# Layer 0's ternary feed-forward: a turn over five batches, the up product scaled on ScalarE, the norm weight on GpSimd

## What is computed

```python
def activation_quant(x):
    s = 127 / clip(max(abs(x), axis=-1), EPS)
    return clip(round(x * s), -128, 127) / s

def weight_quant(w):
    s = 1.0 / clip(mean(abs(w)), EPS)
    return clip(round(w * s), -1.0, 1.0) / s

def bit_linear(x, w):
    return einsum('bsh,oh->bso', activation_quant(x), weight_quant(w))

h = silu(bit_linear(x, w_gate)) * bit_linear(x, w_up)      # 1024 columns
h = ln_weight * (h * rsqrt(mean(h * h) + RMS_EPS))
return bit_linear(h, w_down)                               # 256 columns
```

## Time and profile before

| | |
|---|---|
| median of 3 runs | 3764.42 us (3761.03 to 3766.98) |
| the profiled execution | 3751.3 us, of which its span is 3749.5 |
| busy over the span: PE / DVE / ACT / POOL | 83% / 65% / 43% / 10% |
| mean granted clock of TensorE | 0.91 of full speed |
| tile of the gated product in the stage | first 763.8, last 983.1 us |

### The profile page before, as it was taken

The page is one execution under the profiler, slowest core; times in us unless marked ns, Lnnn a source line. Parts: engine busy times, 40 slices in busy tenths (PEclk is TensorE's granted clock), DMA queues, the critical chain, the costliest instruction groups (busy, mean ns, idle before and its releaser), DMA issues. The chain is left out here.

```text
span 3749.5 us, 77344 instructions
## 1 busy us (share of the span) xinstructions
PE 3113.6 (83%) x28592; PEld 2241.5 (60%) x28592; DVE 2427.6 (65%) x6361; ACT 1617.8 (43%) x3972; POOL 378.5 (10%) x443
## 2 busy tenths in 40 slices
PE   7899999744487898999999999287999679976898
PEld 6566666411265556656666666165887676765786
DVE  6655555588677666666667666776788228856662
ACT  2243444377443455555555555032334224433341
POOL 3000000000042111111111111000110000000110
PEclk9899999855598899999999999598788899999899
DMA  2000000000320000000000000300000000000803
GB/s 99 31 16 23 16 23 15 2 0 0 110 54 2 2 1 3 1 3 1 1 3 1 1 3 1 97 1 6 17 14 9 0 0 1 0 25 21 223 35 105
DMA packets 97026, 90.80 MB, mean 24 GB/s; under 512 B 17680, under 2 KB 85840, under 8 KB 96336
## 3 DMA queue, kind: packets, MB, share of 16 engines
q1 hardware_dynamic: 90656, 79.78, 7.2%
q10 hardware_dynamic: 5808, 7.41, 0.6%
q0 software_dynamic: 384, 1.05, 0.1%
HBM read 79.83 MB, written 8.39 MB: 24 GB/s over the span
## 5 line engine op out<-in xcount | busy, mean ns | idle before, releaser
L3118 PE MATMUL bank<-L1w_w,L1x_xqT 128*128 128x512 f32 x640 | 304.5, 599 | 2.1 <-DVE L1x_xqT L3386 2.1
L3392 DVE TENSOR_REDUCE L1x_ssq<-L1x_square 128x4 f32<-128x512 f32 x192 | 131.5, 685 | 185.7 <-ACT L1x_square L3245 179.8
L1046 DVE TENSOR_REDUCE L0x_top<-bank 128x4 f32<-128x512 f32 x256 | 159.1, 683 | 102.6 <-PE bank L972 99.5
L1031 ACT ACTIVATE L0x_P<-bank,L0x_level 128x512 f32<-128x512 f32 x256 | 155.1, 688 | 156.1 <-PE bank L992 156.1
L3344 POOL TENSOR_TENSOR L1x_square<-L1x_square,L1x_total 128x512 f32<-128x512 f32 x128 | 133.2, 1041 | 603.7 <-DVE L1x_total L3420 603.7
L888 DVE TENSOR_TENSOR x_sb<-x_sb,bank 128x256 f32 (+1 forms) x112 | 47.0, 420 | 223.4 <-PE bank L208 179.9
L3269 ACT ACTIVATE L1x_square<-bank,L1x_top 128x128 f32<-128x128 f32 x512 | 182.0, 375 | 19.7 <-DVE L1x_top L3414 19.7
L3179 PE MATMUL bank<-L1w_wp,L1x_catb 128*128 128x256 bf16 x1536 | 188.4, 273 | 0.1
L3245 ACT ACTIVATE L1x_square<-bank 128x512 f32<-128x512 f32 x192 | 114.8, 598 | 146.8 <-PE bank L3118 146.8
L3118 PEld LDWEIGHTS bank<-L1w_w,L1x_xqT 128*128 128x128 f32 x640 | 115.4, 192 | 99.4 <-issue 95.2
L3179 PEld LDWEIGHTS bank<-L1w_wp,L1x_catb 128*128 128x128 bf16 x1536 | 150.2, 98 | 35.3 <-issue 17.1
(11 more groups left out here) (655 smaller groups left out, 7616.1 us busy)
## 6 DMA issues: line engine op xcount, KB each, us to landing
L0x_mask<-in_maskrows SPq DMA_DIRECT2D x16, 512.0 KB, 3.5
L3f_wgu<-in_L_ffn_Wg SPq DMA_DIRECT2D x8, 704.0 KB, 9.0
L3f_wgu<-in_L_ffn_Wu SPq DMA_DIRECT2D x8, 704.0 KB, 10.2
L1a_wp_quarter<-in_L_xattn_wproj SPq DMA_DIRECT2D x4, 1024.0 KB, 5.6
L3x_ctxT<-in_ctxT SPq DMA_DIRECT2D x32, 128.0 KB, 2.1
L3f_wd<-in_L_ffn_Wd SPq DMA_DIRECT2D x8, 512.0 KB, 9.1
turned_sends<-L3r_sendT ACTq DMA_DIRECT2D x16, 256.0 KB, 2.0
L3e_sends<-turned_sends SPq DMA_DIRECT2D x16, 256.0 KB, 2.9
```

The costliest lines, as they stand in the source:

```text
L1031: act.activation(self.P[:, i % 2, r, :], self.work_bank[r][:, :], ACT.Exp, bias=self.level[:, :]).then_inc(self.p_ready.sem, 1)
L1046: dve.tensor_reduce(self.top[:, s, 16 * c + 4 * r:16 * c + 4 * r + 4], self.work_bank[r][:, :].rearrange("p (h k) -> p h k", h=4), X, ALU.max,
L3118: last = pe.matmul(made_bank[n % 4][:, :], inputs(SOURCE[n], k), w[:, k, 4 * n:4 * n + 4, :], start=(k == 0), stop=(k == C - 1))
L3392: dve.tensor_reduce(ssq[:, 4 * n:4 * n + 4], square[:, (n + 2) % 3, :].rearrange("p (h e) -> p h e", h=4), X, ALU.add).then_inc(sum_ready. ...
```

## The change

TensorE, ScalarE, VectorE and GpSimd now each run `turn(t)` for t from -2 to 17, in which up to five batches (t - 2 to t + 2) are under way. Two turns make a loop's body, four lie on either side.

- VectorE's turn: h of t, the residual of t - 2, the norm and rounding of t - 1, `prepare` of t + 2.
- ScalarE's turn: squares of t, two exponentials and two scaled copies of t + 1, the copy of the turned hq of t - 1, the gate's logarithm (t + 1), the logarithm of the mean square (t), the gate's last exponential (t + 1), the exponential that makes the inverse root (t), and the copy of the turned q of t + 2.
- TensorE's turn: gate and up of t + 1, turning and down product of t - 1, turning of q of t + 2.
- The up product is scaled by ScalarE as it is copied out of its banks. The product with the norm weight is GpSimd's, from h into one of two buffers (`hl`). The root no longer multiplies h: it goes into the scale with which h is rounded and into the largest value. Root and reciprocal become a logarithm and an exponential.
- The sums of absolute weights move to ScalarE, all three in front; the last batch's norm is finished ahead of the weights.

```diff
...
+class TernaryHalves(Ternary):
+
+    def sum_scalar(self, act):
+        act.activation(self.q[:, :, :], self.raw[:, :, :], ACT.Abs, accum_out=self.total[:, :]).then_inc(self.summed, 1)
+    def vector(self, dve, step, out, guard, eps):
+        dve.wait_ge(self.spread, 1)
+        step(dve.tensor_scalar(self.unit[:, :], out, 1.0 / self.count, eps, ALU.mult, guard))
+        step(dve.reciprocal(self.scale[:, :], self.unit[:, :]))
+        step(dve.tensor_scalar(self.raw[:, :, :], self.raw[:, :, :], self.scale[:, :], 1.0, ALU.mult, ALU.min))
+        step(dve.tensor_scalar(self.raw[:, :, :], self.raw[:, :, :], -1.0, ROUND, ALU.max, ALU.add))
+        step(dve.tensor_scalar(self.q[:, :, :], self.raw[:, :, :], ROUND, None, ALU.subtract))
...
-        wg, wu, wd = Ternary(ph, "wg", C, F, weights), Ternary(ph, "wu", C, F, weights), Ternary(ph, "wd", FC, D, weights)
+        wg, wu, wd = TernaryHalves(ph, "wg", C, F, weights), TernaryHalves(ph, "wu", C, F, weights), TernaryHalves(ph, "wd", FC, D, weights)
...
+        unit, unit_g = ph.sb("unit", [128, 2]), ph.sb("unit_g", [128, 2])
+        gate, up, sig, h = (ph.sb(n, [128, F]) for n in ("gate", "up", "sig", "h"))
+        hl = ph.sb("hl", [128, 2, F])
+        ssum, rms, newton = ph.sb("ssum", [128, 2]), ph.sb("rms", [128, 2]), ph.sb("newton", [128, 1])
...
+        gate_exp, gate_log, up_kept = ph.batch_sem("gate_exp", 2), ph.batch_sem("gate_log"), ph.batch_sem("up_kept", 2)
+        product_made = ph.batch_sem("product_made", 2)
...
+        FIRST, LAST = -2, B + 2
+        def turns(eng, turn):
+            for t in range(FIRST, 2):
+                turn(t, t % 2, t)
+            with eng.Fori(0, (B - 4) // 2) as i:
+                for odd in range(2):
+                    turn(i * 2 + (2 + odd), odd, 2 + odd)
+            for t in range(B - 2, LAST):
+                turn(t, t % 2, t)
+        live = lambda t: 0 <= t < B
...
                 if not first:
-                    pe.wait_ge(banks_read.sem, banks_read.after(b - 1))
+                    pe.wait_ge(product_made.sem, product_made.after(b - 1))
...
-            front(0, first=True)
-            with pe.Fori(0, B - 1) as b:
-                front(b + 1)
-                back(b)
-            back(B - 1)
+            def turn(t, odd, at):
+                if live(at + 1):
+                    rise(t + 1, first=(at + 1 == 0))
+                if live(at - 1):
+                    fall(t - 1)
+                if live(at + 2):
+                    turn_q(t + 2)
+            turns(pe, turn)
...
             act.wait_ge(eps_made, 1)
...
+            for w in (wg, wu, wd):
+                w.sum_scalar(act)
...
-            def sigmoid(b):
+            def square(b, odd):
+                act.wait_ge(h_ready.sem, h_ready.after(b))
+                act.activation(sig[:, :], h[:, :], ACT.Square, accum_out=ssum[:, odd:odd + 1]).then_inc(squared.sem, 1)
+
+            def rise(b):
+                act.wait_ge(unit_ready.sem, unit_ready.after(b))
                 act.wait_ge(gate_made.sem, gate_made.after(b))
-                act.wait_ge(unit_ready.sem, unit_ready.after(b))
...
+                    act.activation(gate[:, i * 512:(i + 1) * 512], bank[1 + i][:, :], ACT.Exp, scale=unit[:, 0:1]).then_inc(gate_exp.sem, 1)
+                act.wait_ge(up_made.sem, up_made.after(b))
+                for i in range(2):
+                    act.activation(up[:, i * 512:(i + 1) * 512], bank[3 + i][:, :], ACT.Copy, scale=unit[:, 1:2]).then_inc(up_kept.sem, 1)
+            def gate_logarithm(b):
                 act.wait_ge(gate_exp.sem, gate_exp.after(b))
-                act.activation(sig[:, :], gate[:, :], ACT.Ln, bias=1.0).then_inc(gate_log.sem, 1)
+                act.activation(gate[:, :], gate[:, :], ACT.Ln, bias=1.0).then_inc(gate_log.sem, 1)
+            def square_logarithm(b, odd):
+                act.wait_ge(squared.sem, squared.after(b))
+                act.activation(rms[:, odd:odd + 1], ssum[:, odd:odd + 1], ACT.Ln, bias=rms_eps[:, :], scale=1.0 / F).then_inc(rms_log.sem, 1)
+            def gate_sigmoid(b):
                 act.wait_ge(gate_log.sem, gate_log.after(b))
-                act.activation(sig[:, :], sig[:, :], ACT.Exp, scale=-1.0).then_inc(gate_ready.sem, 1)
-            def batch(b, last=False):
-                act.wait_ge(h_ready.sem, h_ready.after(b))
-                act.activation(square[:, :], h[:, :], ACT.Square, accum_out=ssum[:, :]).then_inc(squared.sem, 1)
-                act.wait_ge(squared.sem, squared.after(b))
-                act.activation(rms[:, :], ssum[:, :], ACT.Sqrt, bias=rms_eps[:, :], scale=1.0 / F).then_inc(rms_ready.sem, 1)
-                if not last:
-                    front(b + 1)
-                    sigmoid(b + 1)
+                act.activation(sig[:, :], gate[:, :], ACT.Exp, scale=-1.0).then_inc(sig_ready.sem, 1)
+            def square_root(b, odd):
+                act.wait_ge(rms_log.sem, rms_log.after(b))
+                act.activation(rms[:, odd:odd + 1], rms[:, odd:odd + 1], ACT.Exp, scale=-0.5).then_inc(rms_ready.sem, 1)
+            def fall(b):
                 act.wait_ge(hq_turned.sem, hq_turned.after(b))
                 act.copy(hqT[:, :, :], bank[5][:, :].bitcast(BF16)).then_inc(hqT_ready.sem, 1)
-            front(0)
+            def turn(t, odd, at):
+                if live(at):
+                    square(t, odd)
+                if live(at + 1):
+                    rise(t + 1)
+                if live(at - 1):
+                    fall(t - 1)
+                if live(at + 1):
+                    gate_logarithm(t + 1)
+                if live(at):
+                    square_logarithm(t, odd)
+                if live(at + 1):
+                    gate_sigmoid(t + 1)
+                if live(at):
+                    square_root(t, odd)
+                if live(at + 2):
+                    keep_q(t + 2)
             pre_norm.scalar(act)
-            sigmoid(0)
-            with act.Fori(0, B - 1) as b:
-                batch(b)
-            batch(B - 1, last=True)
+            turns(act, turn)
...
+        @block.gpsimd
+        def _(pool):
+            weights.wait(pool)
+            def turn(t, odd, at):
+                if live(at):
+                    pool.wait_ge(h_ready.sem, h_ready.after(t))
+                    pool.tensor_tensor(hl[:, odd, :], h[:, :], lnw[:, :], ALU.mult).then_inc(hl_ready.sem, 1)
+            turns(pool, turn)
...
             step = Steps(dve, dve_own)
+            weights.wait(dve)
             dve.memset(rms_eps[:, :], RMS_EPS).then_inc(eps_made, 1)
-            weights.wait(dve)
+            pre_norm.vector(dve)
+            pre_norm.finish(dve)
+            step.restart()
...
+                if at > 0:
+                    step(norm_vector(kit, dve, b, kit.xn[:, :]))
...
+                if at > 0:
+                    dve.wait_ge(q_turned.sem, q_turned.after(b - 1))
+                dve.tensor_scalar(q[:, :], kit.xn[:, :], ROUND, None, ALU.subtract).then_inc(q_ready.sem, 1)
+                if at > 0:
+                    dve.wait_ge(up_kept.sem, up_kept.after(b - 1))
+                step(dve.tensor_scalar(peak[:, :], peak[:, :], 1.0 / 127.0, None, ALU.mult))
+                step(dve.tensor_scalar(unit[:, 1:2], peak[:, :], wu.unit[:, :], -1.0, ALU.mult, ALU.mult))
+                dve.tensor_scalar(unit[:, 0:1], peak[:, :], wg.unit[:, :], -1.0, ALU.mult, ALU.mult).then_inc(unit_ready.sem, 1)
+                step(dve.tensor_scalar(unit_g[:, odd:odd + 1], peak[:, :], wg.unit[:, :], -1.0, ALU.mult, ALU.mult))
+            def product(b, first, odd):
                 if not first:
-                    step(norm_vector(kit, dve, b, kit.xn[:, :]))
-                quantize_vector(dve, step, kit.xn[:, :], q[:, :], peak[:, :], scale[:, :], ALU.max, EPS).then_inc(q_ready.sem, 1)
-                step(dve.tensor_scalar(peak[:, :], peak[:, :], 1.0 / 127.0, None, ALU.mult))
...
+                    dve.wait_ge(hl_ready.sem, hl_ready.after(b - 1))
+                    dve.wait_ge(squared.sem, squared.after(b - 1))
+                for i in range(2):
+                    dve.wait_ge(up_kept.sem, up_kept.after(b, i + 1))
+                    dve.scalar_tensor_tensor(h[:, i * 512:(i + 1) * 512], bank[1 + i][:, :], unit_g[:, odd:odd + 1], up[:, i * 512:(i + 1) * 512], ALU.mult, ALU.mult).then_inc(product_made.sem, 1)
+                dve.wait_ge(product_made.sem, product_made.after(b))
+                dve.wait_ge(sig_ready.sem, sig_ready.after(b))
+                dve.tensor_tensor(h[:, :], sig[:, :], h[:, :], ALU.mult).then_inc(h_ready.sem, 1)
...
-            def batch(b, first=False, last=False):
-                dve.wait_ge(up_made.sem, up_made.after(b))
-                for i in range(2):
-                    step(dve.tensor_scalar(h[:, i * 512:(i + 1) * 512], bank[3 + i][:, :], unit[:, 1:2], -1.0, ALU.mult, ALU.mult))
-                dve.wait_ge(gate_exp.sem, gate_exp.after(b))
-                for i in range(2):
```

(78 more changed lines are left out.)

26 lines of the change are left out of this document (9 added, 17 removed).

## The result

The changed kernel takes 3741.38 us (median, 3737.66 to 3742.55) where the kernel before, in the same series, took 3764.78 (3761.03 to 3766.98): a ratio of 0.9938, 95% interval 0.9923 to 0.9954, so 17 to 29 us less. Its profiled execution took 3741.98, of which 3740.2 is its span.

A forecast was written before the change was run, and what follows sets the result against it. A ring of waits, 13.54 us a turn against 14.62, was to bound the stage, not VectorE's 11.6. Terms 0.9 - 0.5 + 4.1 + 1.2 + 14.0 - 6.1 - 1.3 = 12.3 us saved gave a 3752 median, range 3738 to 3764.

The forecast's parts named there:

- the rival of TensorE's upper level: TensorE's clock at its upper level: transposes 0.62 against 1.03, 0.4 us less in each of 15 turns; 3744, chance 0.12.
- a ring of 13.54: Loop of waits through VectorE, TensorE and ScalarE from one gated product to the next: 13.54 us against 14.62 before.
- its five steps: Gated product 1.20, residual and statistics 0.98, quantize to TensorE's start 4.33, transposes 1.07, ScalarE's copy to exponential 5.96 us.
- ScalarE's cover: ScalarE's spare time each turn before the turned hq arrives for its copy: 1.8 us.
- Table loads: Two a turn, both on the waiting path; its rival, one table set, has VectorE bound at 11.6: 3720, chance 0.05.
- GpSimd's hold: VectorE's first two-input Newton operation waits for GpSimd's norm-weight product to end: 0 to 0.27 us a turn, taken as 0.1.
- weights: Stage's preparation: weight sums leave VectorE for ScalarE, 20.9 us instead of 21.78, 0.9 saved.
- fill, to the first product: Before the first gated product: scaled copies add 1.4 us, last batch's norm and root leave the path (0.9): 0.5 lost.
- turn 0: First turn, with no hq and so no relay of waits: 10.5 us, 4.1 saved.
- thirteen turns, with the hold: Remaining turns of the loop at 1.08 us saved each, 14.0, less 1.3 in all for VectorE held by GpSimd.
- The slower case: GpSimd's product holds VectorE: gain gone at 3.1 us of product, 3773 at 3.7 us; chance 0.06.
- Waits not costed: Three waits of 0.16 plus GpSimd's upper end: +0.4 us a turn, 3758; chance 0.22 together with no change.

The follow-up runs named there:

- run with one table: Changed kernel with one table holding both logarithm and exponential, loaded once ahead of the turns: 3713.61 us, ratio 0.9870; read for its time alone.
- repetition: The kernel before and the changed kernel, both unchanged, measured and profiled a second time: 3762.13 us and 3741.26 us, ratio 0.9944 for the changed kernel.

## Why the prediction was right, and where it was not

**What the forecast hit.** 3741.4 lies inside the range stated, 3738 to 3764, but not in the part that was held most likely, 3746 to 3757 (a chance of 0.55). It lies where the rival of TensorE's upper level had been put, and that rival explains at most 1.5 us of it. So the mechanism of the stage was forecast, and that the total still fell into the range is in part luck.

**The bound: right.** The kernel was forecast not to run at VectorE's 11.6 us a turn but at a ring of 13.54. The turn above is 873.11 - 859.60 = 13.51, and its five steps are 1.15, 0.96, 4.36, 1.07 and 5.97 against 1.20, 0.98, 4.33, 1.07 and 5.96. That this ring bounds, and that VectorE's work lies behind it, was shown by removing two different parts of it: the loads, and the copy. Either leaves a beat of 11.30 with no idle time before the gated product. The forecast turn of 13.3 to 13.8 is that of the loop, 13.50 to 13.59. ScalarE's cover was somewhat larger than forecast, about 2.2 us for 1.8.

**Table loads: right for this kernel.** Two a turn, placed as in the earlier trace rows. The Trainium skill ("ScalarE: Activation LUTs", section "Table sets: the hidden batching unit") says that one set holds both functions. The run with one table agrees in so far as no load followed its own; since its output differed, it doesn't show that this stage's functions are right from that set. The forecast said that only the page spoke for this rival. It overlooked the kernel before itself, whose L1x (layer 1's second stage) loads the same table by an instruction of its own; its logarithms (L3250) and exponentials (L3252, L3269) then run for 1097 us without another load:

```profile
1240.45 1.28 ACT L3314 ACT_TABLE_LOAD   x1
...
1242.90 0.29 ACT L3250 ACTIVATE L1x_inv<-L1x_ssq,L1w_floor 128x4 f32<-128x4 f32 x1
1243.23 0.20 ACT L3252 ACTIVATE L1x_inv<-L1x_inv 128x4 f32<-128x4 f32 x1
...
2338.73 1.28 ACT L273 ACT_TABLE_LOAD   x1
```

So the earlier trace rows show where loads stand when the program asks for no table, and not that they are needed wherever a logarithm meets an exponential. In this stage the same table gave other values; why, no run here shows.

**GpSimd's hold: the mechanism right, its place in the sum wrong.** The product took 2.36, the upper end of the earlier trace rows; the first Newton operation took 0.33 in the loop, to the product's end (860.91 + 2.36 = 863.27, 862.95 + 0.33 = 863.28), so 0.17 a turn within the bounds 0 to 0.27. In turn 1, which has no residual, the operation took 1.29, a hold of 1.13 (0.8 forecast). The Trainium skill ("SBUF — State Buffer", section "Who interferes with whom") says that an operation with at most one input from SBUF, outside the two-port modes, does not contend, and that one with two does, with a GpSimd operation that reads SBUF. The runs agree: 0.21 and 1.29 for the same multiplication in the two forms. An operation with one tensor that was held stands in the last section.

**The terms.** What the stage gained, by the sum's own parts:

| term | forecast | measured |
|---|---|---|
| weights | +0.9 | +1.6 |
| fill, to the first product | -0.5 | -1.3 |
| turn 0 (10.14 us) | +4.1 | +4.5 |
| turn 1 (13.51 us) | +1.2 | +1.1 |
| thirteen turns, with the hold | +14.0 - 1.3 = +12.7 | +15.0 |
| drain | -6.1 | -5.7 |
| stage, unrounded | +12.3 | +15.3 |

- Weights: ScalarE's sums of 128x2048 took 1.91, 1.89 and 1.89 and were done after 5.8 us, where two passes of the 1024-wide row and an estimated read had given 6.9.
- Fill: of the last batch's norm and root I took 0.9 off the path. It had not been on it: before, ScalarE's root ended (756.45) as TensorE finished the gate product, and only the two scaled copies (762.10 to 763.38) were new there.
- Turn 0 and the thirteen turns are both counted against the mean step before, 14.62, as the forecast did. Before's own turn 0 took 13.69 and its loop's turns 14.70, so against its like turn 0 gained 3.6 and the thirteen 15.9; the sum is the same.
- Thirteen turns: the term that was sized wrong is the hold as a term of its own, 0.1 a turn on top of 13.54. Turns whose transposes took 1.03 are 13.50 to 13.59, 13.55 in the middle, with a hold of 0.17 inside. Without it, maximum to transposes took 4.19 where 4.33 had been added up (the estimated wait of 0.06 was not there), and the product's step 1.15 for 1.20. 0.09 less in nine turns is 0.8 us. The other 1.5 are the last four turns, 13.44, 13.31, 13.17 and 13.17, whose transposes took 0.97, 0.77, 0.62 and 0.62. So the rival of TensorE's upper level did come, for these turns alone; in the 100 us of the loop shown above the granted clock was 0.50, below the 0.57 of before.

**From the stage to the kernel: the step that failed.** The forecast took the 13 us between profiled execution and median as constant and put the median of after at 3739 + 13 = 3752. The profiled execution of before was one with a short rest (3479.2 us outside the stage; 3488.0 in its repetition), the profiled execution of after lay at its median. Between the two profiled executions there are only 9.3 us, since 5.9 of the stage's 15.3 were taken by the rest. So 3741.4 lies 11 below the forecast: 3 from the stage's terms, and 8 from the surplus of the medians, of which the repetition shows 3.6.

**The rivals.** The slower case was a hold of GpSimd's with a product over 3.1 us; the product was 2.36 and the hold 0.17. Doubled, it made the kernel 0.2% slower than before, so the mechanism of this rival is real, from a point that a single product did not reach. Waits not costed: VectorE's 0.88 at the loop's end is there in every other turn, inside idle time; it cost nothing until the ring was gone.

## What to carry to other kernels

When work is spread over engines that had been unevenly loaded, add up the new relay as well as the busiest engine: here the engines were 73% busy and the stage ran at the sum of five waits, which could be added up from rows of the old trace to 0.2 us a turn or better. What breaks such a relay is often not a faster instruction but its place: a copy behind the exponential instead of ahead of the logarithm was worth 17 us, the scaling moved to another engine nothing. Two fixes may be worth 1 us each alone and 16 together, when one uncovers the wait that the other removes.

## What the runs showed of the hardware

Not only operations with two tensors were held. In turn 0 of after a `tensor_scalar` of 128x256 with one tensor, 0.35 us in every other turn, took 1.30 and ended 0.16 after GpSimd's product:

```profile
769.58 2.38 POOL L2105 TENSOR_TENSOR L0f_hl<-L0f_h,L0f_lnw 128x1024 f32<-128x1024 f32 x1 [636.35 <-DVE L0f_h L2150]
...
770.82 1.30 DVE L2130 TENSOR_SCALAR xn<-xn,L0f_scale 128x256 f32<-128x256 f32 x1
```

Under the product of other turns and kernels the maximum over 128x1024 took 1.20, the statistics 0.43 and the 128x1 operations with per-partition operands 0.21, as without it. So the number of tensors alone doesn't tell which operation is held; what sets this one apart, no run here shows. The rounding add is a `tensor_scalar` of this kind; in every order tried here it starts after the product's end, and what it would do under it was not tried.
